# Second cross attention of a perceiver: the weighted sum moved behind the next scores, the softmax shares one sequence ahead

## The reference, cut to what matters

```
q = (x @ Wq.T).reshape(b, t, h, s)          # 16 heads of 8
k_ = (context @ Wk.T).reshape(b, tc, h, s)  # tc = 257
v = (context @ Wv.T).reshape(b, tc, h, s)
dot = jnp.einsum('bthd,bchd->bhtc', q * inv4, k_ * inv4)
attn = jax.nn.softmax(dot, axis=-1)
out = jnp.einsum('bhtc,bchd->bthd', attn, v).reshape(b, t, e)
return out @ Wo.T + bo
```

## Time and profile before

| what | value |
|---|---|
| median of 3 runs | 1579.08 us (1574.88 to 1580.87) |
| profiled execution, its own time | 1572.63 us |
| its span | 1570.8 us |
| scores of this pass (L1495) | 640.1 to 1141.8 us |
| TensorE in 640 to 1150 us | busy 473.74 of 510 us, granted clock 1.00 |
| VectorE, ScalarE, GpSimd in 700 to 800 us | 77.64, 73.36, 60.74 of 100 us |

### The profile page before, as it was taken

The page is one execution under the profiler, slowest core; times in us unless marked ns, Lnnn a source line. Parts: engine busy times, 40 slices in busy tenths (PEclk is TensorE's granted clock), DMA queues, the critical chain, the costliest instruction groups (busy, mean ns, idle before and its releaser), DMA issues. The chain is left out here.

```text
span 1570.8 us, 48801 instructions
## 1 busy us (share of the span) xinstructions
PE 1264.7 (81%) x15330; PEld 1097.8 (70%) x15331; DVE 996.1 (63%) x3247; ACT 841.9 (54%) x2658; POOL 835.7 (53%) x1700
## 2 busy tenths in 40 slices
PE   3877788989729996799999999999969878449991
PEld 2655777878629886577777777777758767349991
DVE  4655367877346664577777777777759888433334
ACT  1555256565314443577777777777737665224450
POOL 2555024666636564466666666666534566646661
PEclk9999578788559998899999999999979999569996
DMA  7998552121112121312111111111000000122215
GB/s 223 261 263 218 213 165 76 58 63 53 35 49 73 59 62 37 113 62 91 33 50 33 50 34 43 40 37 43 15 15 3 16 24 23 45 61 68 70 58 169
DMA packets 91997, 122.01 MB, mean 78 GB/s; under 512 B 12689, under 2 KB 67218, under 8 KB 91858
## 3 DMA queue, kind: packets, MB, share of 16 engines
q1 hardware_dynamic: 74194, 82.77, 17.8%
q0 software_dynamic: 12288, 34.82, 7.4%
q10 hardware_dynamic: 5376, 2.63, 0.6%
HBM read 89.68 MB, written 30.49 MB: 76 GB/s over the span
## 5 line engine op out<-in xcount | busy, mean ns | idle before, releaser
L1592 ACT ACTIVATE p_prob<-six,p_nm 128x257 f32<-128x257 f32 x512 | 236.4, 475 | 132.1 <-DVE p_nm L1634 122.2
L1634 DVE TENSOR_REDUCE p_nm<-six 128x2 f32<-128x514 f32 x256 | 164.8, 686 | 12.9 <-PE six L1495 12.8
L1842 PE MATMUL bank<-sb_w,m_experts_aT 128*128 x1152 | 156.6, 279 | 7.6 <-ACT m_experts_aT L1871 4.9
L1821 POOL DMA_INDIRECT expert_outputs<-m_experts_y,m_experts_dest x144 | 142.7, 991 | 25.9 <-POOL m_experts_tiny L1820 11.4
L1858 PE MATMUL six<-m_experts_xT,m_experts_w 128*128 128x128 f32 x1152 | 156.0, 279 | 0.0
L1516 PEld LDWEIGHTS six<-sb_const,p_prob 128*128 128x128 f32 x1024 | 109.5, 141 | 65.5 <-issue 59.1
L1516 PE MATMUL six<-sb_const,p_prob 128*128 128x128 f32 x1024 | 137.0, 277 | 19.3 <-issue 17.5
L1842 PEld LDWEIGHTS bank<-sb_w,m_experts_aT 128*128 128x128 f32 x1152 | 141.1, 193 | 13.0 <-issue 12.8
L776 POOL DMA_INDIRECT expert_inputs<-p_r_x,p_r_slot x128 | 126.0, 984 | 41.2 <-issue 34.5
L1375 POOL TENSOR_TENSOR p_score<-p_score,p_mx 128x512 f32<-128x512 f32 x64 | 67.2, 1049 | 147.8 <-DVE p_mx L1320 145.9
L1858 PEld LDWEIGHTS six<-m_experts_xT,m_experts_w 128*128 128x128 f32 x1152 | 143.3, 196 | 0.6 <-issue 0.2
(11 more groups left out here) (287 smaller groups left out, 3498.2 us busy)
## 6 DMA issues: line engine op xcount, KB each, us to landing
ctxN_ring<-ctxN POOLq DMA_DIRECT2D x32, 516.0 KB, 10.6
ctxT_ring<-ctxT SPq DMA_DIRECT2D x32, 514.0 KB, 12.4
p_ctxT<-ctxT SPq DMA_DIRECT2D x32, 514.0 KB, 3.6
m_experts_x<-expert_inputs SPq DMA_DIRECT2D x144, 64.5 KB
bd_scores<-p_rows SPq DMA_DIRECT2D x32, 256.0 KB, 2.8
p_bd<-bd_scores SPq DMA_DIRECT2D x32, 256.0 KB
sb_w<-w SPq DMA_DIRECT2D x32, 256.0 KB
p_y<-expert_outputs SPq DMA_DIRECT2D x32, 128.0 KB, 3.3
```

The costliest lines, as they stand in the source:

```text
L1592: last = nc.scalar.activation(prob[:, b, g, :], scores_ps[:, g, 0:CTX], ACT.Exp, bias=nm[:, b % 2, g:g + 1], accum_out=total[:, b % 2, g:g ...
L1634: nc.vector.tensor_reduce(nm[:, b % 2, g:g + 2], scores_ps[:, g:g + 2, 0:CTX], AX.X, ALU.max, negate=True).then_inc(s[most], 1)
L1821: nc.gpsimd.indirect_dma_start(m.ys_dram[:, :], bass.IndirectOffsetOnAxis(ap=dest[:, t.par:t.par + 1], axis=0), y[:, t.par, :], None).then ...
L1842: last = nc.tensor.matmul(ps[6 + t.two][:, 0:D], aT[:, t.two, f * P:(f + 1) * P], m.w2[:, DS(held[p] + f * D, D)], start=(f == 0), stop=(f ...
```

## The change

No arithmetic changes and no instruction is added or removed; every engine's program in this pass is written in another order.

- TensorE: in each step, behind `scores` of sequence i now comes `weigh` of i-2, then `turn_probs` of i-1, keys and values of i+2, and `shares` of i-1 (was i-2), and last what is done once per tile. `bank_read` is split into `before_weighing` and `before_shares`; the latter waits for `masked` of i-2 (was i-3), in step 1 also for `end_v` (was step 2), and in step 2 for `q`.
- ScalarE: the copy `pT_a` comes ahead of the copy of keys and values.
- VectorE: reciprocal of i-1 first, then z (step 0), zT (step 1) or the addition to x (step 3), then `largest`, then `take_share` and `finish` of i-2 (was i-3, and ahead of `largest`), `end_v` (now step 1) and `q_all` (step 2), then `pT_b`, then statistics.
- GpSimd: `spread` of i-1 comes ahead of the work on x in steps 0 and 1.

```
@@ TensorE
+            def before_weighing(at, b):
                 if b == 1 and at(2).live:
                     pe.wait_ge(s["zT"], at(2).nth())
+                if b == 3 and at(4).live:
+                    pe.wait_ge(tail.x_new, at(4).nth())
+            def before_shares(at, b):
+                t, u = near(at, b, -2)
+                if t.live:
+                    pe.wait_ge(s["masked"], seq(t, u))
+                if b == 1 and at(4).live:
+                    pe.wait_ge(s["end_v"], at(4).nth())
                 if b == 2 and at(2).live:
                     pe.wait_ge(s["q"], at(2).nth())
...
                     if cur.live:
                         scores(cur, b)
+                    before_weighing(at, b)
+                    t, u = near(at, b, -2)
+                    if t.live:
+                        weigh(t, u)
                     t, u = near(at, b, -1)
                     if t.live:
                         turn_probs(t, u)
                     t, u = near(at, b, 2)
                     if t.live:
                         keys_and_values(t, u)
-                    t, u = near(at, b, -2)
-                    bank_read(at, b)
+                    before_shares(at, b)
+                    t, u = near(at, b, -1)
                     if t.live:
                         shares(t, u)
...
-                    if t.live:
-                        weigh(t, u)
@@ VectorE
-                    t, u = near(at, b, -3)
+                    t, u = near(at, b, -1)
                     if t.live:
-                        take_share(t, u)
-                        finish(t, u)
-                    if b == 2 and prev.live:
...
+                        dve.wait_ge(s["exp_b"], seq(t, u))
+                        if past(t, u, 2):
+                            dve.wait_ge(s["spread_share"], seq(t, u, 2))
+                        nc.vector.reciprocal(recip[:, u % 2, :], total[:, u % 2, :]).then_inc(s["recip"], 1)
...
+                    if cur.live:
+                        largest(cur, b)
+                    t, u = near(at, b, -2)
+                    if t.live:
+                        take_share(t, u)
+                        finish(t, u)
+                    if b == 1 and prev.live:
...
@@ GpSimd
                     done, u = near(at, b, -1)
+                    if done.live:
+                        pool.wait_ge(s["recip"], seq(done, u))
...
+                                                ALU.mult).then_inc(s["spread"], 1)
                     t = at(1)
                     if b == 0 and t.live:
```

More of the change, by code:

```diff
@@ L1518, in turn_probs @@
                 last.then_inc(s["pT_ps"], 1)
-            def bank_read(at, b):
-                t, u = near(at, b, -3)
+            def before_weighing(at, b):
+                if b == 1 and at(2).live:
+                    pe.wait_ge(s["zT"], at(2).nth())
+                if b == 3 and at(4).live:
+                    pe.wait_ge(tail.x_new, at(4).nth())
+            def before_shares(at, b):
+                t, u = near(at, b, -2)
                 if t.live:
                     pe.wait_ge(s["masked"], seq(t, u))
-                if b == 1 and at(2).live:
-                    pe.wait_ge(s["zT"], at(2).nth())
+                if b == 1 and at(4).live:
+                    pe.wait_ge(s["end_v"], at(4).nth())
                 if b == 2 and at(2).live:
                     pe.wait_ge(s["q"], at(2).nth())
[L1529 to L1532, removed]
             def shares(t, b):
@@ L1595, in steps @@
                         last.then_inc(s["exp_b"], 1)
+                    t, u = near(at, b, -1)
+                    if t.live:
+                        act.wait_ge(s["pT_ps"], seq(t, u))
+                        if past(t, u, 2):
+                            act.wait_ge(s["o_ps"], seq(t, u, 2))
+                        nc.scalar.activation(pT[:, u % 2, 0:2], turned_ps[0], ACT.Copy).then_inc(s["pT_a"], 1)
                     t, u = near(at, b, 2)
@@ L1602, in steps @@
                                              ACT.Copy).then_inc(s["kv"], 1)
[L1603 to L1608, removed]
             over_tiles(act, 4, steps)
@@ L1660, in steps @@
                         nc.vector.tensor_scalar(zT[:, nxt.par, :], misc_ps, s0, None, ALU.mult).then_inc(s["zT"], 1)
+                    if b == 3 and prev.live:
+                        dve.wait_ge(s["y_ps"], prev.nth())
+                        dve.wait_ge(s["xb"], prev.nth())
+                        nc.vector.tensor_tensor(m.X[:, prev.cols()], misc_ps, xb[:, prev.par, :],
+                                                ALU.add).then_inc(tail.x_new, 1)
+                    if cur.live:
[5 more added lines that the diff above has]
+                    if b == 1 and prev.live:
+                        if prev.past(2):
+                            dve.wait_ge(s["y_ps"], prev.before(2))
+                        nc.vector.tensor_tensor(
+                            end_v[:, prev.par, :].rearrange("p (b i) -> p b i", b=B4), end_ps.rearrange("p (b i) -> p b i", b=B4),
+                            m.last_values[:, prev.cols(B4)].unsqueeze(2).broadcast_to([P, B4, LEN]),
+                            ALU.mult).then_inc(s["end_v"], 1)
                     if b == 2 and nxt.live:
@@ L1669, in steps @@
                             ALU.mult).then_inc(s["q"], 1)
[L1670 to L1676, removed]
                     t, u = near(at, b, -1)
                     if t.live:
[L1679 to L1682, removed]
                         dve.wait_ge(s["pT_ps"], seq(t, u))
@@ L1715, in steps @@
                     done, u = near(at, b, -1)
+                    if done.live:
+                        pool.wait_ge(s["recip"], seq(done, u))
+                        if past(done, u, 2):
+                            pool.wait_ge(s["o_ps"], seq(done, u, 2))
+                        nc.gpsimd.tensor_tensor(spread[:, u % 2, 0],
+                                                recip[:, u % 2, :].unsqueeze(2).unsqueeze(3).broadcast_to([P, G, H4, HD]),
+                                                mine, ALU.mult).then_inc(s["spread_share"], 1)
+                        pool.wait_ge(s["spread_share"], seq(done, u))
+                        nc.gpsimd.tensor_tensor(spread[:, u % 2, 1], spread[:, u % 2, 0],
+                                                prob[:, u, :, LAST].unsqueeze(2).unsqueeze(3).broadcast_to([P, G, H4, HD]),
+                                                ALU.mult).then_inc(s["spread"], 1)
                     t = at(1)
@@ L1730, in steps @@
                         nc.gpsimd.tensor_tensor(xb[:, prev.par, :], m.X[:, prev.cols()], m.bX[:, :], ALU.add).then_inc(s["xb"], 1)
[L1731 to L1741, removed]
                     if b == 2 and at(1).live:
```

## The result

| | before | after |
|---|---|---|
| median of 10 runs each | 1578.88 us | 1594.63 us (1588.19 to 1603.87) |
| ratio | | 1.0097, 95% interval 1.0075 to 1.012 |
| span of the profiled execution | 1570.8 us | 1586.4 us |
| a tile, by turns | 15.90 and 15.83 us | 16.24 and 16.73 us |
| granted clock in the steady part | 1.00 | 1.00 |

The change makes the kernel 1% slower, 15.75 us; 17.5 had been forecast. The pass, from its first to its last `scores`, takes 501.4 us before and 517.3 after, 15.9 more. What lies ahead of it and behind it, where no code differs, is 5.7 us shorter and 5.4 longer in the two profiled executions; the stretch ahead alone takes between 636.9 and 642.3 us in experiments 5 to 8, so this is taken as scatter.

A forecast was written before the change was run, and what follows sets the result against it. In each step the loop over the single set of score banks (3.67 us) competes with TensorE's own sequence. Two tiles +1.17, 30 tiles +17.5 us: 1579.1 becomes 1596.6, forecast 1591 to 1605, outer range 1580 to 1610.

The forecast's parts named there:

- Step 1: TensorE's transposes: the 0.29 us wait for `pT_a` goes, and the step falls from 3.94 to the score banks' 3.67, -0.27.
- Step 2: `shares` on TensorE waits for `q_all` until 3.29 us into the step, which takes 4.16 against 4.34, -0.18.
- Steps 3 and 0: `shares` waits for GpSimd's `spread`, behind closing work starting 0.45 us later: 8.35 against 7.51 (+0.84), 8.89 against 7.66 (+1.23).
- the 6.73: Time in us behind the scores of step 3 at which step 0 now wants `shares` of sequence 3.
- One guess beside this chain: VectorE's statistics in step 3: another GpSimd load may cause their 0.16 us pause; without it the chain is 0.12 shorter.
- The sum: Two tiles +1.17 us, +0.58 a tile; over the 30 tiles with both neighbours, +17.5 us.
- Bounds: Orders on TensorE the trace lacks: `weigh` behind `scores`, transposes behind `weigh`; 0.64 us taken from the nearest rows.
- The rival with a pause of 0.21 at each change of TensorE's mode: Step 1 on TensorE takes 3.86 us in place of 3.65: +6 us, 1602; 12 in 100.
- The rival of no change: GpSimd's chain gets 0.4 to 0.6 us shorter as gaps and the statistics' pause shrink: +1 to +6, 1583; 15 in 100.
- The faster rival: GpSimd's `spread` is in time, so steps 3 and 0 take 3.67 us each: -21 us, 1558; 8 in 100.

The follow-up runs named there:

- experiments 5 to 8: Four runs: kernel before plus two small GpSimd products, 1.0014; changed kernel with keys' copy first, 1.0101; changed kernel with both layouts early, 0.9913; that plus early statistics, 0.993.
- experiment 3: Kernel before with only ScalarE's two copies exchanged, transposed probabilities ahead of keys and values: ratio 0.9923 to the kernel before.
- Experiment 2: Changed kernel with VectorE's statistics of step 3 directly behind the maxima, ahead of share, masked and the copy: ratio 0.9916 to the kernel before.
- 1: Changed kernel with GpSimd's layout of a tile's last sequence in step 3, ahead of the closing work: ratio 0.9999 to the kernel before.
- experiment 4: Changed kernel with two more one-column GpSimd products behind the closing work, results unused: ratio 1.0158 to the kernel before.
- 5: Kernel before with two more one-column GpSimd products behind the closing work, results unused: ratio 1.0014 to the kernel before.
- 7: Changed kernel with the last sequence's layout ahead of the closing work and the first's ahead of the operations on x: ratio 0.9913 to the kernel before.
- experiment 9: Changed kernel with VectorE's maxima back behind share, masked, `end_v` and q; single run: 1704.37 us, ratio 1.084 to the kernel before.

## Why the prediction was right

- **Step 1, -0.27.** 3.68 after, -0.26. The reading behind it (0.29 of hidden waiting for `pT_a`) is shown by experiment 3, where the exchange of the two copies alone closes the gap.
- **Step 2, -0.18.** 4.20 after, -0.15. `shares` starts 3.30 behind the scores (902.69 to 905.99), forecast 3.29, and the rest of the step takes 0.89, forecast 0.87.
- **Steps 3 and 0, +0.84 and +1.23.** 3.67 + 4.69 = 8.36 and 3.67 + 5.18 = 8.85, against 7.51 and 7.66: +0.85 and +1.19. The chain in parts: statistics 0.47 later (0.45), `shares` 7.85 and 8.34 behind the scores (7.86 and 8.40), so 1.12 and 1.61 late by the 6.73 (1.13 and 1.67). The rows name less, 0.99 and 1.28, since TensorE gets there by itself only 6.86 and 7.06 behind the scores, the latter at the loop's turn. The second is 0.06 less, for the most part because it takes 3.18 from the first closing operation to the last keys (877.83 to 881.01), where it took 3.28. Experiment 2 shows the chain's start as the lever, 1, 4 and 5 its queue. One guess beside this chain does not hold: the pause of 0.16 inside the statistics stays (894.06 to 894.22) while GpSimd stands idle, so it needs no load there.
- **The sum.** Two tiles 32.97 against 31.73, +1.24, forecast +1.17. Over the pass it came to 15.9 us. I had counted 15 steady pairs of tiles where there are 12: these cost 15.0 us together, the four tiles ahead of them 0.4 less than before (step 0 takes 3.66, 4.21 and 4.47 in the second, third and fourth), the four behind them 1.25 more. So the number came out as near as it did partly by luck: a pair had been put 0.07 too low and the count of pairs too high.
- **Bounds.** That `weigh` behind the scores and transposes behind `weigh` cost nothing beyond their own time is seen in the rows: 0.65 and 0.57. The rival with a pause of 0.21 at each change of TensorE's mode falls, by these rows and by experiment 3. The Trainium skill ("TensorEngine Tiling (Array Packing)", Key Properties) states that a change of tiling mode drains TensorE. No row here shows a pause for it: `weigh` and the transposes start before the modelled ends of what is ahead of them, 0.72 and 0.64 after its start. What a drain costs inside these distances the trace does not tell.
- **The rival of no change** wanted the gaps between GpSimd's closing operations and that pause to shrink. Both stayed: 2.74 and 3.18 from the first of them to the last keys.
- **The faster rival** had the right mechanism and lacked the move: experiments 2 and 7 bring the layout in time and give 0.84 and 0.87% (13 us) where 21 us (1.3%) had been worked out. The difference is step 0 at 3.73 to 4.01 and step 3 at 3.92 in one tile, in place of 3.67.

## What to carry to other kernels

Taking a consumer one step forward saves nothing unless its producer's whole queue can follow: look at what is written ahead of the producer on its engine, at the step where once-per-tile work stands, and add the delay of that work's own input. An engine that is busy six tenths, as GpSimd here, can be the one that is late. A constant short gap with "issue" beside it, present in some steps and absent in one, is worth comparing with the ends of the other engines' instructions: here it was a wait of 0.3 us that an exchange of two copies removed, for 0.8% of the time.

## What the hardware showed that I had not expected

TensorE's granted clock fell in experiment 4. In three tiles of the steady part step 1 took 5.3 us in place of 3.68. The stretches around one of them (columns: window; its length; busy time and instructions of TensorE, its weight loads, VectorE, ScalarE, GpSimd; granted clock; DMA share; GB/s):

```profile
core 0: us, PE busy (x) PEld busy (x) DVE busy (x) ACT busy (x) POOL busy (x), PEclk, DMA share, GB/s
893.00:900.00 7.00, 5.28 (x69) 3.79 (x68) 4.17 (x13) 4.21 (x14) 5.04 (x16) 0.97 0.00 0
900.00:903.00 3.00, 3.00 (x18) 2.64 (x12) 2.29 (x8) 2.54 (x9) 2.17 (x5) 0.50 0.00 0
903.00:910.00 7.00, 6.89 (x83) 5.38 (x83) 4.71 (x14) 3.71 (x12) 2.70 (x8) 1.00 0.30 94
```

The granted clock is 0.50 for these 3 us, the 1.2 GHz level, and the eight transposes take 1.97 us in place of 1.09. Ahead of it stands a step 0 of 5.25 us, in which TensorE waited 1.49 for the layout. The changed kernel, whose steps 0 take 5.18 (5.24 once), has no such tile, and its granted clock is 1.00 from 700 to 1090 us. The three falls cost 4.8 us, nearly half of what the two small operations cost there.

It is tempting to say that the longer wait brought the clock down. The runs do not bear that out as a rule: in experiment 4 the clock fell behind three of the twelve steps 0 of 5.25 us or more and stayed at 1.00 behind the other nine, and in experiment 9, where TensorE waits 1.1 us in the mean ahead of 100 of the scores and is busy 75% of the pass, the granted clock is 1.00 but for one place (0.71 from 1054 to 1058 us, in a step 0 of 5.37 in place of 5.07). What decides it is not shown. What is shown is that a kernel with a wait in every tile can lose 1.6 us more in some of its tiles, behind the wait.
